# Filler products in a recurrence, and an activation table loaded one step sooner

## The reference, cut to what matters

```
x = x + ga * rwkv6(norm(x))          # layer 0: decay scan over 1024 tokens, 2 heads of 64
x = x + gb * moe0(norm(x))           # 16 experts, each token goes to its best one
x = x + ga * hla(norm(x))            # layer 1: second-order linear attention, 16 heads of 32
x = x + gb * moe1(norm(x))           # 4 live experts of width 704, each token goes to two:
                                     # (silu(x w1) * (x w3)) w2
```

## Time and profile before

| what | value |
| --- | --- |
| three runs | 695.73, 697.32, 701.44 us |
| median | 697.32 us |
| the profiled execution | 697.54 us |
| its span, first to last instruction | 695.4 us |
| PE busy in it | 644.1 us, 93% |
| DVE busy | 421.8 us, 61% |
| ACT busy | 302.6 us, 44% |
| POOL busy | 254.6 us, 37% |
| mean granted clock of TensorE | 0.955 of 2.4 GHz |

### The profile page before, as it was taken

The page is one execution under the profiler, slowest core; times in us unless marked ns, Lnnn a source line. Parts: engine busy times, 40 slices in busy tenths (PEclk is TensorE's granted clock), DMA queues, the critical chain, the costliest instruction groups (busy, mean ns, idle before and its releaser), DMA issues.

```text
span 695.4 us, 26343 instructions
## 1 busy us (share of the span) xinstructions
PE 644.1 (93%) x10928; PEld 550.0 (79%) x10928; DVE 421.8 (61%) x1384; ACT 302.6 (44%) x1017; POOL 254.6 (37%) x387
## 2 busy tenths in 40 slices
PE   5799999889849988999999999999998999999995
PEld 4476666667739977888888888888876999998995
DVE  3667677877544435577777776868675554444443
ACT  1446566544005514545554455545443353333231
POOL 2355566556540031122435252524243432222225
PEclk9769899999669999999999999999999999999999
DMA  7999000000018510000000000000311556566472
GB/s 191 304 318 292 17 3 2 3 2 17 24 51 257 147 45 10 8 7 8 20 11 19 12 19 14 17 15 12 117 54 26 197 189 242 204 235 222 144 242 61
DMA packets 50485, 65.68 MB, mean 94 GB/s; under 512 B 5168, under 2 KB 40208, under 8 KB 47424
## 3 DMA queue, kind: packets, MB, share of 16 engines
q1 hardware_dynamic: 44992, 57.22, 26.3%
q0 software_dynamic: 2912, 6.03, 2.6%
q10 hardware_dynamic: 2464, 0.76, 0.5%
HBM read 49.45 MB, written 18.87 MB: 98 GB/s over the span
## 4 chain that ended last, share of the span: by engine, by line
PE 56%; DVE 3%; DMA 2%; issue 1%; POOL 1%; ACT 0%; SPq 0%; DVEq 0%; POOLq 0%
PE quad L1765 6%; PE bank L1907 6%; PE quad L1889 5%; PE quad L1891 5%; PE bank L1790 4%; PE pair L1727 3%; PE bank L1813 3%; PE quad L1771 2%; PE bank L1816 2%; PE pair L1729 2%; PE pair L1728 2%; PE bank L1823 2%; PE bank L1826 2%; PE pair L1752 2%; DMA f_xg<-moe_slots 2%; PE bank L1909 1%
## 5 line engine op out<-in xcount | busy, mean ns | idle before, releaser
L2163 DVE TENSOR_TENSOR h_masked<-quad,const 128x1536 f32<-128x1536 f32 (+2 forms) x66 | 112.6, 1705 | 59.8 <-PE quad L1771 54.0
L2001 ACT ACTIVATE f_sa<-quad 128x256 f32<-128x256 f32 (+1 forms) x115 | 40.2, 351 | 93.7 <-PE quad L1891 75.7
L2277 DVE TENSOR_TENSOR f_hid<-f_sa,quad 128x256 f32<-128x256 f32 (+1 forms) x115 | 43.0, 379 | 53.4 <-ACT f_sa L2001 53.3
L2381 POOL DMA_INDIRECT moe_slots<-g_pay,g_slot x28 | 28.9, 1032 | 77.2 <-PE bank L1835 68.7
L1889 PE MATMUL quad<-f_xT,wall 128*128 128x256 f32 (+1 forms) x190 | 50.8, 350 | 2.7 <-DVE f_hid L2277 2.7
L1907 PE MATMUL bank<-wall,f_hid 128*128 128x128 f32 x390 | 50.7, 277 | 1.1 <-DVE f_hid L2280 0.9
L1907 PEld LDWEIGHTS bank<-wall,f_hid 128*128 128x128 f32 x390 | 47.8, 192 | 3.6 <-DVE f_hid L2280 2.8
L1891 PE MATMUL quad<-f_xT,wall 128*128 128x256 f32 (+1 forms) x190 | 49.9, 344 | 0.0
L1978 ACT ACTIVATE h_gT<-bank 128x128 f32<-128x128 f32 x64 | 17.8, 278 | 66.6 <-PE bank L1816 66.6
L1765 PE MATMUL quad<-h_qk 32*128 32x128 f32 x1024 | 46.5, 296 | 0.3 <-DVE h_masked L2163 0.3
L1765 PEld LDWEIGHTS quad<-h_qk 32*128 32x128 f32 x1024 | 34.3, 185 | 9.5 <-issue 7.0
(11 more groups left out here) (412 smaller groups left out, 1792.7 us busy)
## 6 DMA issues: line engine op xcount, KB each, us to landing
wall<-moe_w SPq DMA_DIRECT2D x23, 1088.0 KB, 5.1
moe_slots<-blank SPq DMA_DIRECT2D x2, 2112.0 KB, 25.0
wall<-in_experts_dram SPq DMA_DIRECT2D x1, 4120.0 KB, 22.6
e_w<-in_experts_dram SPq DMA_DIRECT2D x15, 257.5 KB, 3.0
moe_slots<-blank SPq DMA_DIRECT2D x1, 1984.0 KB, 9.4
moe_slots<-e_yg SPq DMA_DIRECT2D x7, 256.0 KB, 3.7
f_xg<-moe_slots SPq DMA_DIRECT2D x12, 132.0 KB, 4.1
moe_w<-in_moe_w_dram SPq DMA_DIRECT2D x1, 1408.0 KB, 7.9
```

Of the source, the lines that this page charges most:

```text
L2001: act.activation(sa[g % 3][:, 0:s], up_bank(n, f)[:, 0:s], ACT.Silu).then_inc(f_sa, 1)
L2163: dve.tensor_tensor(masked[k % 4][:, :, a * P:z * P], quad[:, :, a * P:z * P], cst("causal")[:, None, a * P:z * P].to_broadcast([P, HPG, ( ...
L2277: dve.tensor_tensor(hid[n % 2][:, f, 0:s], sa[g % 3][:, 0:s], up_bank(n, f)[:, T1:T1 + s], ALU.mult)\
L2381: pool.indirect_dma_start(out=t["moe1_slots"], out_offset=bass.IndirectOffsetOnAxis(ap=slot[:, b * 2 + k:b * 2 + k + 1], axis=0), in_=pay[ ...
```

## The change

In the recurrence of layer 0 PE gets a second helper, `keep_on`, which is `keep_busy` into bank 5 (columns of the chunk's output that are free there). One product stands inside `project(i + 1)` before the wait for xx, one after `mix(i + 1)`; in chunk 7 two stand in its place. Chunk 6 gets two more before mix, chunk 5 three before the wait for att, and the drain begins with four into bank 3. That makes 16 + 9 = 25 products. In chunk 0 PE also waits for `s_cross`, DVE's clearing of that bank at the start.

At the seam ACT does `warm`, silu(0, 0) and silu(0, 1) in step 9, and silu(0, 2), silu(0, 3) in step 10. DVE does gate_in(0, 0) in step 9 before it takes the count, and gate_in(0, 1) before table(). DVE's waits of steps 9 and 10 for sums that it doesn't use are dropped.

```diff
@@ project(n), PE
+                if n:
+                    keep_on(1)
                 pe.wait_ge(s_xx, n * MIXES + 3)
@@ PE
+            def keep_on(count):
+                for _ in range(count):
+                    pe.matmul(bank[5][:, 0:N], cst("ident"), const[:, 0:N], start=True, stop=True)
@@ step(i, ...), PE
+                if i == CHUNKS - 2:
+                    keep_on(2)
                 if i >= 2:
                     pe.wait_ge(s_rlg, i - 1)
...
                 if prepare:
                     mix(i + 1)
+                    if i == 0:
+                        pe.wait_ge(s_cross, 1)
+                    keep_on(1)
+                else:
+                    keep_on(2)
                 pe.wait_ge(s_diag, i * 4 + 4)
...
+                if i == CHUNKS - 3:
+                    keep_on(3)
                 pe.wait_ge(s_att, i * 4 + 4)
@@ drain(n, q), PE
+                keep_busy(4, 3)
                 transpose_h(n - 1)
@@ layer 1, ACT
-                if (i, k) == (CHUNKS - 1, PER + 2):
+                if (i, k) == (CHUNKS - 1, PER + 1):
                     act.activation(warm[:, :], cst("ones")[:, 0:1], ACT.Silu)
                     silu(0, 0)
                     silu(0, 1)
+                if (i, k) == (CHUNKS - 1, PER + 2):
+                    silu(0, 2)
+                    silu(0, 3)
...
-                    if n or f > 1:
+                    if n or f > 3:
                         silu(n, f)
@@ layer 1, DVE
-                if live(i, k, -3):
+                if live(i, k, -3) and (live(i, k, -1) or live(i, k, -3, LAST)):
                     dve.wait_ge(s_right, now - 2)
                     dve.wait_ge(s_oc, now + 1)
...
                 if (i, k) == COUNT:
+                    gate_in(0, 0)
                     dve.wait_ge(s_cnt, 1)
...
             steps(dve, step)
             z = CHUNKS - 1
+            gate_in(0, 1)
             table()
...
             for n in range(NT):
-                gate_in(n, 0)
-                gate_in(n, 1)
                 if n:
+                    gate_in(n, 0)
+                    gate_in(n, 1)
                     result(n - 1)
```

More of the change, by code:

```diff
@@ L2173, in step, with gate_in @@
                         .then_inc(s_tab, 1)
+            def gate_in(n, f):
+                g, s = block_of(n, f), halves(n) * P
+                dve.wait_ge(f_sa, g + 1)
+                if f == 0 and n >= 2:
+                    dve.wait_ge(f_down, before(n - 1))
+                if f < FULL1:
+                    dve.tensor_tensor(hid[n % 2][:, f, 0:s], sa[g % 3][:, 0:s], up_bank(n, f)[:, T1:T1 + s], ALU.mult)\
+                        .then_inc(f_hid, 1)
+                else:
+                    dve.tensor_tensor(hid[n % 2][0:TAIL1, f, 0:s], sa[g % 3][0:TAIL1, 0:s], up_bank(n, f)[0:TAIL1, 0:s],
+                                      ALU.mult).then_inc(f_hid, 1)
             def early_table():
```

## The result

The changed kernel takes 686.14 us (median of six runs, 684.28 to 687.73), the one before 697.26 beside it (six runs, 695.73 to 701.44): a ratio of 0.983, with a 95% interval from 0.980 to 0.987. That is 11.1 us where the forecast was 6.5, and 1.4 us under the lower end of the range. Measured again later, it took 687.63 us against 699.49, ratio 0.983 [0.979, 0.988]. The profiled execution took 684.28 us, with a span of 682.2.

The account below looks back on a forecast made before the run. In full-clock chunks PE waits for ACT and POOL; in half-clock chunks, the drain and the seam PE's slow clock is on the path. 697.54 + 0.8 (slow chunks) - 3.7 (drain) - 3.6 (seam) = 691.0 us, range 687.5 to 695.5.

Parts of the forecast that it names:

- Fillers in full-clock chunks: Chunks 1 and 3 to 7: added products lie in PE's waits and cost nothing; outer end 5.4 us.
- first rival: Drain: the clock falls there all the same and the drain gains nothing, 694.7 us in all; chance 0.18.
- Fillers in slow chunks, +0.8: Chunks 0 and 2, where PE is the bound: nothing for chunk 0, 0.87 us for chunk 2; upper end 3.5.
- the rival by which the front gains: Front: the 1.54 us hole or the slow stretch behind it goes, 3.0 us more gained, 687.2 us; chance 0.13.
- The drain, -3.7: Drain: four products fill PE's 2.17 us wait for h, full clock holds, output product comes 3.7 us sooner.
- the end without loss: Drain: the best end of its range, -3.9 us, with no handoff lost.
- the one by which the fillers are paid at half clock: Chunks 0, 2 and the drain's start: fillers cost 4.8 us, the seam gives 3.6, 698.7 us; chance 0.05.
- The seam, -3.6: Seam: earlier table load and gating cut PE's hole from 2.70 to 0.6 us at full clock; down(0) 3.8 sooner, 3.6 taken.
- Tile 2's rows: Behind the seam: rows expected at 541.7, PE asks at 542.2; close, with half a microsecond at stake.
- the added drain of the Trainium skill: Seam: about 1.38 us more per switch of table sets would leave a gain of 2.2 us, 692.4 in all.
- The sum: Whole kernel: profiled 697.54 us plus 0.8, less 3.7 and 3.6, gives 691.0 us; chance of the forecast 0.54.

Follow-up runs that it names:

- seam alone: The kernel before with only the change's edits to ACT and DVE at the seam, no added product: median 695.83 us, ratio 0.999.
- drain alone: The kernel before with only the four products added at the start of the drain: median 697.58 us, ratio 0.996.
- the chunks' products alone: The kernel before with only the products added in the chunks, without the drain's four and the seam's edits: median 694.72 us, ratio 0.994.
- the five more in the front: The changed kernel with sixteen more products behind the drain's last ranks and five more ahead of chunk 0: median 687.41 us, ratio 0.985.
- sixteen at the end of layer 0: The changed kernel with sixteen more products behind the drain's last ranks, in PE's wait there: median 688.17 us, ratio 0.984.

## Why the prediction was wrong

**Fillers in full-clock chunks: the step that failed.** "I take nothing." For the cost that is right in chunks 3 and 4, 17.17 us with and without: the holes cover it. In chunk 1, which was put at nothing too, the pair costs 0.2 to 0.9 us (17.1 to 17.7 against 16.8 to 16.9). What was missed is the gain. Chunks 3 to 7 of the kernel before are not full-clock chunks. Even the execution that the forecast was made from has two short dips there, in chunks 6 and 7, which the prediction doesn't name (stretches as in the earlier trace rows):

```profile
152.00:154.00 2.00, 2.00 (x5) 0.92 (x6) 1.90 (x7) 0.70 (x2) 2.00 (x5) 0.50 0.00 0
172.00:175.00 3.00, 3.00 (x12) 2.59 (x12) 2.63 (x14) 0.67 (x3) 2.18 (x3) 0.50 0.13 44
```

They cost that execution nothing, and other executions lose more. The six profiles with PE's old stream up to the drain (three of before, seam alone, drain alone, and the changed kernel without chunk products) have a mean of 99.0 us from chunk 2's state to h(6); with the products it is 94.9. That is 4.1 us on the average, and nothing in the profile used. I looked for the slow clock where the trace showed it, instead of where it may come: at every chunk's two holes. The sign was there: the runs of before lay 5.7 us apart, and the prediction itself says, in its first rival, that the dips may lie elsewhere in each execution. It gave that no term in the sum.

**Fillers in slow chunks, +0.8.** Small and not the cause. In chunk 0 the pair shows no price: its state product comes at 45.1 us in the mean of nine profiles with the pair, at 45.2 in seven without. Chunk 2 has no gain from its pair: 18.2 us in the mean of seven profiles without, 18.9 in ten with, in a scatter of 7 us. What goes with its length is the hole marked "issue": it stood at 70.6 to 72.8 us in twelve of the eighteen profiles, with 0.72 to 1.95 us, and chunk 2 then took 17.6 to 24.4 us; in the six others, the first profile of the changed kernel among them, chunk 2 took 17.2. So the rival by which the front gains named nearly the right time, 687.2, for a wrong reason. What the two first profiles showed there was the chance of two executions.

"Issue" says only that no engine explains the hole. The DMA packets of the traces show more. Queue q8 brings instructions, 1.43 MB in 87 loads in the first profile of before, which is one load for some 250 of PE's 21,856 matmuls and weight loads. In all twelve profiles the hole ends 1.36 to 1.62 us after such a load has landed, in the first profile of before at 72.84, behind a load from 70.19 to 71.36. That is how a wait of PE for its next instructions would look. No run moved a load, so the cause isn't shown.

**The drain, -3.7.** Right. The four lie in the wait, the clock holds from h(6) to h(7) in all eleven profiles that have them, and in none of the seven that don't: h(6) to h(7) is 11.2 us against 12.95 to 16.24. In the forecast's own pair of profiles it is 4.17: 3.9 to the output product, the whole of what I gave as the end without loss, and 0.3 behind it. The rival by which the clock falls there all the same didn't happen, though its condition, a longer wait, came about; nor did the one by which the fillers are paid at half clock.

**The seam, -3.6.** Right, step by step. Counted from the first up product, I had the table's start at 3.0 us, its end at 7.8 and down(0) at 10.0; measured 2.9, 7.6 and 9.84. The hole of PE is 0.45 us (0.6 expected), and 3.96 us come back, in eleven profiles to 0.02. Tile 2's rows aren't late, and the gain stays: from down(0) to the end it is 153.8 us in both profiles. The warm-up starts 0.02 us behind the load's row, so the added drain of the Trainium skill ("ScalarE: Activation LUTs", "What ACT_TABLE_LOAD costs") doesn't show here either. Where the clock happens to hold at the old seam, as in the run without the seam's edits (12.12 us), the edits are worth only 2.3.

**The sum, mended.** The profiled execution of before had lost 3.4 us in chunk 2 and 0 in chunks 3 to 7; the six profiles lose 1.1 and 4.1 in the mean. By these two stages a typical execution is 697.5 - 2.3 + 4.1 = 699.3 us, at the upper end of the medians of before in the five sets of runs (697.3 to 699.5). The change takes 4.1 + 4.2 + 4.0 from it and adds 0.5 in chunk 1 and 0.7 in chunk 2: 11.1 us less, 688.2. Measured are 11.1 and 11.9 less, 686.1 and 687.6.

What stays open: the seam alone and the drain alone gave less in the total (2 us and 0.3 by the medians) than in their own stages. Their sum with the chunks' products alone is some 5.5 us by the medians and 8.0 by the ratios, of the 11 to 12 that they give together. Adding the chunks' products gave 3.2 us, undoing them cost 5 to 7. The scatter of kernels that lose the clock by chance is large enough for much of that, but it isn't shown that it is all: the stretch from layer 0's experts to the first up product, which holds none of the edits, lies between 320.5 and 324.4 us in the eighteen profiles. Why the extras of chunks 5 and 6 are worth 3 to 5 us isn't shown either.

## What to carry to other kernels

A profile shows where the slow clock fell in one execution; if the runs scatter by more than the stages you mean to mend can explain, take two or three more profiles before you call a stage a full-clock one, and count PE's holes instead of the dips. A filler that costs nothing in a hole is not one that is worth nothing. Where a kernel scatters, undo one part of the finished version besides adding one part to the old one: here that told more (some 2.5 to 9 us against 0 to 3), though the versions with a part undone spread over 7 to 11 us themselves. And compare stages: those where the clock held agree to 0.1 us in a few profiles, while medians of totals leave 3 us open.

## What the runs showed of the hardware

Where in the recurrence the clock falls belongs to the execution, not to the program alone: with the same instructions up to chunk 0 the clock first fell at 16.8 us in one profile, at 17.4 in another, and between 24.0 and 27.3 in the others (29.6 with the five more in the front). The granted clock was 1.00 or 0.50 there, full speed or half. That agrees with the Trainium skill, "TensorE: Matmul & The Clock Gate", section "What's actually happening", by which the activity monitor runs freely and isn't reset when a kernel starts.

In chunk 3 of the kernel before, the clock fell at 93.4 us in one execution, behind holes of 0.57 and 0.49 us, and didn't fall in another behind holes of 0.57 and 0.50. With a row of 0.70 us in place of each, no fall came in chunks 3, 4 and 5 in any of ten profiles. Why one execution falls there and another doesn't is not shown.

Products issued behind a fall were dear: sixteen at the end of layer 0 took 9.66 us, and the pair in a fallen chunk 2 has rows of 1.22 us each instead of 0.70. The drain's four, issued while the clock was full and ahead of the wait, took 1.95 us, and the clock held behind them.

The hole marked "issue" in chunk 2 belongs to the execution too: 1.54 us in two of three profiles of the kernel before and 0.32 in the third, 24.3 us of chunk behind one of 1.00 us and 17.8 behind one of 0.99. With the pairs of chunks 0 to 2 ahead of it, it still came in six profiles of ten.
